# Feed forward with Hadamard steps: the last pass of the norm on ScalarE, its bias from GpSimd

## The reference

```python
def _layernorm(x, axis=-1, eps=1e-05):
    m = jnp.mean(x, axis=axis, keepdims=True)
    v = jnp.var(x, axis=axis, keepdims=True)
    return (x - m) / jnp.sqrt(v + eps)
...
def _L1_ffn_ref(x, w_gate, w_up, w_down):
    ...
    def bitlinear(x, w):
        return jnp.einsum('bsh,oh->bso', act_quant(x), weight_quant(w))

    def h_bitlinear(x, w):
        return jnp.einsum('bsh,oh->bso', act_quant(fwht(x)), weight_quant(w))
    gate = bitlinear(x, w_gate)
    up = bitlinear(x, w_up)
    intermediate = jax.nn.silu(gate) * up
    return h_bitlinear(intermediate, w_down)
...
x = _layernorm(x + _L1_ffn_ref(x, L1_ffn_w_gate, L1_ffn_w_up, L1_ffn_w_down), axis=-1)
```

## Time and profile before

| | |
|---|---|
| median of 3 runs | 5197.23 us (5192.73 to 5197.41) |
| profiled execution, its time | 5189.15 us |
| profiled execution, its span | 5187.9 us |
| mean granted TensorE clock | 0.927 of full speed |
| instructions | 65674 |
| GpSimd L1700 in the stage | 64, mean 2590 ns |
| VectorE L266 in the stage | 16, mean 2131 ns |

### The profile page before, as it was taken

The page is one execution under the profiler, slowest core; times in us unless marked ns, Lnnn a source line. Parts: engine busy times, 40 slices in busy tenths (PEclk is TensorE's granted clock), DMA queues, the critical chain, the costliest instruction groups (busy, mean ns, idle before and its releaser), DMA issues. The chain is left out here.

```text
span 5187.9 us, 65674 instructions
## 1 busy us (share of the span) xinstructions
PE 4484.8 (86%) x22935; PEld 2381.3 (46%) x23000; DVE 3016.7 (58%) x5466; ACT 1676.3 (32%) x3306; POOL 1693.8 (33%) x1860
## 2 busy tenths in 40 slices
PE   7996888899999668887999898849999997996688
PEld 6773222244445544553333333325555554443466
DVE  5885777668868977883555556533323333555422
ACT  1112766522113315662222222201222211453332
POOL 1223222100117853551011113555555554112311
PEclk9997999999997778999999999879999998998699
DMA  4330000100000011000011110039999987001000
GB/s 139 98 92 12 2 2 2 72 17 1 1 0 1 1 51 72 1 1 29 31 35 56 29 49 18 25 83 228 236 235 233 219 192 184 2 1 46 2 15 19
DMA packets 154390, 327.67 MB, mean 63 GB/s; under 512 B 25841, under 2 KB 39665, under 8 KB 152498
## 3 DMA queue, kind: packets, MB, share of 16 engines
q1 hardware_dynamic: 106370, 222.50, 13.2%
q0 software_dynamic: 46976, 100.56, 10.0%
q10 hardware_dynamic: 720, 0.40, 0.0%
HBM read 377.91 MB, written 79.30 MB: 88 GB/s over the span
## 5 line engine op out<-in xcount | busy, mean ns | idle before, releaser
L205 PE MATMUL ps<-arena 128*128 128x512 f32 (+19 forms) x18679 | 3930.9, 453 | 415.2 <-ACT arena L1786 54.0
L205 PEld LDWEIGHTS ps<-arena 128*128 128x128 f32 (+6 forms) x18744 | 1856.2, 165 | 2293.3 <-issue 1215.2
L210 PE MATMUL ps<-arena 128*128 128x128 f32 (+2 forms) x3232 | 424.1, 271 | 249.8 <-DVE arena L266 52.2
L210 PEld LDWEIGHTS ps<-arena 128*128 128x128 f32 (+2 forms) x3232 | 346.0, 140 | 425.6 <-issue 194.6
L2877 POOL DMA_INDIRECT moe_y<-arena x191 | 304.9, 1596 | 298.7 <-DVE arena L2846 243.8
L256 POOL TENSOR_SCALAR arena<-arena 128x1 f32<-128x1 f32 x160 | 54.6, 341 | 985.7 <-DVE arena L250 983.9
L2406 ACT ACTIVATE arena<-ps 128x1024 f32<-128x1024 f32 (+3 forms) x256 | 166.3, 701 | 580.6 <-PE ps L205 571.6
L867 DVE TENSOR_REDUCE arena<-ps 128x2 f32<-128x1024 f32 x256 | 303.9, 1218 | 86.0 <-PE ps L205 85.3
L2432 DVE TENSOR_REDUCE arena<-ps 128x2 f32<-128x256 f32 (+3 forms) x256 | 198.9, 820 | 257.8 <-PE ps L205 257.8
L2829 DVE SCALAR_TENSOR_TENSOR arena<-ps,arena 128x128 f32<-128x128 f32 x382 | 103.6, 313 | 410.3 <-ACT arena L2816 344.7
L841 ACT ACTIVATE arena<-ps 128x512 f32<-128x512 f32 x512 | 277.6, 597 | 129.2 <-PE ps L205 124.2
(11 more groups left out here) (310 smaller groups left out, 3946.8 us busy)
## 6 DMA issues: line engine op xcount, KB each, us to landing
arena<-in_L_ffn_gu SPq DMA_DIRECT2D x191, 768.0 KB
arena<-in_L_ffn_dn SPq DMA_DIRECT2D x191, 256.0 KB
arena<-in_L_ffn_dn SPq DMA_DIRECT2D x191, 128.0 KB
arena<-in_L_ffn_w SPq DMA_DIRECT2D x64, 256.0 KB
moe_y<-arena SPq DMA_DIRECT2D x34, 256.0 KB
arena<-in_L_ffn_w_gate SPq DMA_DIRECT2D x32, 256.0 KB
arena<-in_L_ffn_w_up SPq DMA_DIRECT2D x32, 256.0 KB
arena<-in_L_ffn_w_down SPq DMA_DIRECT2D x32, 256.0 KB
```

What stands on the lines that cost most here:

```text
L205: return self.nc.tensor.matmul(out, lhsT, rhs, start=start, stop=stop, skip_group_check=True)
L210: return self.nc.tensor.transpose(out, in_, ident[0:n, 0:n])
```

## The change

In `l1_ffn`, VectorE no longer makes the last pass of the norm. In its part down it makes z and the statistics alone. GpSimd, after the power, makes the negated mean and its product with the power (two 128 x 1 instructions into the new small tile MR). ScalarE has a new part norm with a lag of 5 at the end of its order, which waits for GpSimd's product and writes k.X as scale times z plus bias.

```diff
--- before.py
+++ after.py
@@ -1672,7 +1672,7 @@
     YT = [k.alloc([16, P], BF16) for _ in range(2)]
     SG = [k.alloc([512]) for _ in range(3)]
     sm = k.alloc([NT, 12])
-    MG = k.alloc([2])
+    MG, MR = k.alloc([2]), k.alloc([4, 2])
     moe_place(k)
     ZERO = k.alloc([512])
     early = k.W - 4104
@@ -1681,7 +1681,7 @@
     sc = k.bsc
     HN = float(1.0 / np.sqrt(2048))
 
-    LAG = dict(quant=0, turn=1, up=2, up2=2, hadamard=3, stats=4, scale=4, clip=4, down=5)
+    LAG = dict(quant=0, turn=1, up=2, up2=2, hadamard=3, stats=4, scale=4, clip=4, down=5, norm=5)
 
     def order(names):
 
@@ -1742,7 +1742,7 @@
                 t.then_inc(*pe.done("y", i))
 
     def scalar():
-        for what, i in order("hadamard scale down up clip up2 turn quant"):
+        for what, i in order("hadamard scale down up clip up2 turn quant norm"):
             m = sm[:, i, :]
             if what == "turn":
                 act.wait_ge(pe, "xt", i)
@@ -1785,6 +1785,11 @@
                     act.wait_ge(pe, "y", i - 2)
                     nc.scalar.activation(YT[i % 2][:, 8 * c:8 * c + 8, :], eighths(R.of("yt", i, c)), ACT.Copy).then_inc(
                         *act.done("yt", i, c))
+
+            elif what == "norm":
+                act.wait_ge(pool, "root", i)
+                nc.scalar.activation(k.X[:, i, :], k.zb[i % 4], ACT.Identity, bias=MR[:, i % 4, 1:2], scale=k.mv[:, i % 4, 3:4]
+                                     ).then_inc(*act.done("x", i))
 
     def vector():
         for what, i in order("quant stats hadamard clip down up"):
@@ -1838,10 +1843,11 @@
             elif what == "down":
                 dve.wait_ge(pe, "y", i)
                 dve.wait_ge(dve, "fz", i)
-                dve.wait_ge(dve, "x", i - 4)
+                dve.wait_ge(act, "x", i - 4)
                 nc.vector.scalar_tensor_tensor(out=k.zb[i % 4], in0=R.of("y", i), scalar=m[:, 6:7], in1=k.X[:, i, :], op0=ALU.mult,
                                                op1=ALU.add).then_inc(*dve.done("z", i))
-                k.norm(i)
+                dve.wait_ge(pool, "root", i - 4)
+                k.norm_stats(i)
 
     def gpsimd():
         nc.gpsimd.memset(ZERO, 0.0).then_inc(*pool.done("zero"))
@@ -1856,7 +1862,13 @@
                 butterfly(nc.gpsimd.tensor_tensor, i, 3, ALU.add).then_inc(*pool.done("b3", i))
                 butterfly(nc.gpsimd.tensor_tensor, i, 3, ALU.subtract).then_inc(*pool.done("b3", i))
             elif what == "down":
+                pool.wait_ge(act, "x", i - 4)
                 k.norm_rstd(i)
+                nc.gpsimd.tensor_scalar(MR[:, i % 4, 0:1], k.mv[:, i % 4, 0:1], -1.0, 1.0, ALU.mult, ALU.mult).then_inc(
+                    *pool.done("mean", i))
+                pool.wait_ge(pool, "mean", i)
+                nc.gpsimd.tensor_tensor(MR[:, i % 4, 1:2], MR[:, i % 4, 0:1], k.mv[:, i % 4, 3:4], ALU.mult).then_inc(
+                    *pool.done("root", i))
 
     def loads():
         for a, n in zip(k.early2, "qk"):
```

## The result

The kernel after takes 5238.89 us (median of 4 runs, 5233.07 to 5241.97), the kernel before beside it 5194.98 us (4 runs, 5191.08 to 5197.41). The ratio is 1.0082, with a 95% interval from 1.0070 to 1.0094: slower by 43.9 us. The forecast was 5229.8 us in a range from 5218 to 5247, so 32.6 us of growth; the sign and the loop that the prediction names held, the size was 11 us short, and a part of the growth came from the clock, which the prediction had argued away.

What follows compares the result with a forecast made beforehand. The prediction took TensorE's loop of 20.50 us as the bound, replaced after the change by one through GpSimd's butterflies; 28.8 us in the steps + 3.8 at the end = 32.6, so 5197.2 + 32.6 = 5229.8 us, range 5218 to 5247.

Steps and rivals of the forecast that it cites:

- The bound and the removal: Steady step of layer 1's feed forward: TensorE's loop sets 20.50 us; removing VectorE's L266, 2.4 us, is worth nothing.
- TensorE's loop: Steady step of 20.50 us: last product, transposes, Hadamard matmuls, L1766, L1771, L1786, down and up matmuls, product again.
- The loop through P: ScalarE's norm waits for GpSimd's product after the butterflies, delaying L1762 and Hadamard matmuls: 2.45 us longer, step 22.95 us.
- P: The end of GpSimd's block of four butterflies in a step, at 2140.49 in the steady step read.
- How often: Steps 5 to 17 lengthen: 22.1 us in nine, 6.4 us in three, 0.35 us in step 5; 28.8 us together.
- rival 3: TensorE's clock falls in the longer holes, once a step in 12 steps: 20.5 us on top, 5250 us; chance 5%.
- The tail: At the stage's end, tile 14's norm delays L1786 of tile 15 by 3.34 us; stage ends 3.8 us later.
- The sum: Whole kernel: 28.8 + 3.8 = 32.6 us of growth, giving 5229.8 us, 0.63% slower.
- Rival 2: ScalarE never waits for GpSimd; only its 0.72 us pass counts, 0.50 a step: 9.8 us, 5207 us; chance 5%.

## Why the prediction was right, and where its sizes were off

**The bound and the removal.** Right. The step hung on TensorE's loop, the last product waits 0.31 us for TensorE before and after, and taking the pass away alone changes nothing (1.0008).

**The loop through P.** Right, and close in size. The forecast step was 22.95 us with the power at 0.88 us; where the clock plays no part it is 22.92 (the kernel with both holes filled), with the power at 0.95. The terms that went into it were off in opposite directions: the matmul starts 0.63 us after L1762, not 0.89; the scaling follows 0.08 us behind the power's end, not 0.04 ahead of it; the Hadamard matmuls take 3.84 us, not 3.74.

**How often.** Here one claim failed: that the quantizing passes keep their distance from P and L259 its 0.88 us in nine steps. L259 takes 0.94 or 0.95 us in four of them and 0.55 in five. Four of those five steps are 0.4 us shorter; the last of them, the ninth after the first norm, is so by only 0.25, since there the scaling takes 0.34 us instead of 0.19. In four of the five TensorE's down and up block had run slow (11.5 to 12.0 us): the loop's slack of 2.4 us hides these 1.7, but the last product and with it the quantizing come later, behind GpSimd's small instructions. In that ninth step no block was slow: VectorE's quantizing pass starts 0.01 us ahead of L259, where in the four with the long L259 it is 0.03, and whether so little decides it is not shown. With both holes filled no such block is slow, and L259 keeps its place as forecast.

**The clock.** The step that failed for size is the argument against rival 3. It said that with no hole above 2.92 us the clock stays at the upper level. Holes of 1.89 to 2.16 us were enough: in four steps the Hadamard matmuls behind them ran partly at the lower level, 1.2 GHz (granted clock 0.50 from 2170.50 to 2172.20 us), and took 5.46 us instead of 3.84, and there nothing hides it. A row of the kernel before could have warned: its first down and up block with a norm, of 47 matmuls, took 11.99 us from 2085.69 after the same hole of 2.92 us, and its step was 22.19 us; I read steady steps only. So forecast and rival 3 came true together. Rival 3 had a fall in each of twelve steps; it came in four. Nothing in the prediction says how many it would be, so that the time stayed inside the range owes something to luck: twelve times 1.62 us are 13 us more than four times, some 5252 us, beyond the range's end of 5247. Over the twelve intervals the growth is 32.6 us where the sum had 28.5. Four slow Hadamard blocks add 4 x 1.62 = 6.5, the power at 0.55 us in five steps takes off 2.0, and the small terms above some 0.4. The first interval grew by 0.35 us (22.19 to 22.54), exactly as forecast; together 32.9 us against 28.8.

**The tail.** Forecast 3.8 us, measured 6.5: the order of events was right, and L1786 of tile 15 came 4.1 us later against the butterflies (3.3 were forecast), 0.6 of it from slower matmuls of tile 14 (6.26 against 5.63 us). The matmuls of tile 15, after a hole of 4.42 us, took 5.09 us instead of 3.40. I had named this with a price of up to 3.5 and taken none; 1.7 would have been the better value.

**The sum.** Inside the stage 32.9 + 6.5 = 39.4 us, and the stage measures 39.3 more, where I had 32.6. The remaining 4.6 of the 43.9 us lie outside; in the two profiled executions alone, which are 52.8 us apart, it is 13.5. Behind the stage all kernels here have the same instructions, and that part took 2799.1 us in the profile of the kernel before, 2814.4 in the first of the kernel after and 2797.3 in its second. In that second profile the stage is 39.4 us longer than before and the rest is no longer at all. The interval of the whole difference, 36 to 49 us, holds the 39.3 as well. So the 39 us of the stage repeat, and a remainder outside it is not shown to belong to the change.

**Rival 2** fell: in every step L1762 starts behind P, and ScalarE waited 39.9 us for GpSimd's product, in 12 places. The waits are not the steady 1.9 us of the forecast, though. In the steps that still quantize they are 1.9 to 2.2 us behind a down and up block at the full clock, and 0.4 us or nothing behind a slow one, which makes ScalarE itself late.

## What to carry to other kernels

A step moved to another engine costs what it makes the queue behind it wait for, not what it takes: put it where its input is a step old and the engine is idle, and the same instructions cost next to nothing. The busiest engine is not the bound while its last gating instruction still waits for another; follow the loop, and after each change look for the loop that comes next. And count a new hole in TensorE's work twice, once as time and once as a chance of the lower clock behind it.

## What the runs showed of the hardware

TensorE's clock fell to its lower level behind holes of 1.9 to 3.7 us in some steps and not in others with the same hole: 47 matmuls in 10.31 or 11.99 us after 2.92 us of idling, in the same kernel. It fell behind the hole and not in it: in the kernel after the granted clock was 1.00 in the hole from 2166.60 to 2168.78 us, 0.74 in the next 1.72 us of matmuls and 0.50 in the 1.70 us after these. With steps of exactly 20.50 us it nearly never fell (in none of twelve steps of the kernel before behind its first); with steps of 20.66, 21.7 or 22.5 us it fell in a good part of them; with both holes reduced to 0.4 us it did not fall at all. The kernel before thus ran in a favourable rhythm, and each lengthening of its step tried here with the holes left open cost more than the lengthening itself. What decides in which step the clock falls is not shown.

VectorE's one-input pass over 512 values takes 0.5 us alone, 2.5 us where it starts 0.8 us into one of GpSimd's butterflies of 2.6 us and 0.99 us where it starts some 0.1 us before the next begins. Four butterflies together lose 0.07 us to it in the first case and 0.18 in the second (10.41 against 10.34 us, 10.74 against 10.56).
